# Low-rank projection of layers 1 and 3 with its weights stationary in two fp32r parts, in a four-layer convolution and feed-forward kernel

## The reference, cut to what matters

```python
x = x + _L0_ffn_ref(_L0_cond_ref(x, cond, ...), A, B, Wr, br)
x = x + _L1_ffn_ref(_L1_cond_ref(x, cond, ...), gate, kernel, bias, lora_A, lora_B, lora_A_shared, lora_B_shared)
x = x + _L2_ffn_ref(_L2_cond_ref(x, cond, ...), base_W, gate_W, lora_A, lora_B)
x = x + _L3_ffn_ref(_L3_cond_ref(x, cond, ...), W, b, A, Bmat, LiMEs)

def _L1_ffn_ref(x, gate, kernel, bias, lora_A, lora_B, lora_A_shared, lora_B_shared):
    base_out = jnp.matmul(x, kernel) + bias
    A_eff = jnp.einsum('bn,nri->bri', gate, lora_A)        # 32 columns, chosen by group of 4 samples
    B_eff = jnp.einsum('bn,nor->bor', gate, lora_B)
    Ax = jnp.einsum('bri,bti->btr', A_eff, x_flat)
    delta_flat = jnp.einsum('bor,btr->bto', B_eff, Ax)
    Ax_s = jnp.einsum('ri,bti->btr', lora_A_shared, x_flat)  # 32 columns, shared
    delta_flat = delta_flat + jnp.einsum('or,btr->bto', lora_B_shared, Ax_s)
    return base_out + delta_flat

def _L3_ffn_ref(x, W, b, A, Bmat, LiMEs):
    H = jnp.einsum('btd,od->bto', x, W) + b
    z = jnp.einsum('btd,dr->btr', x, A)                    # 32 columns
    ...                                                    # routing weights p_mix from H, z and LiMEs
    return H + jnp.einsum('btr,ro->bto', z * p_mix, Bmat) * scaling
```

## Time and profile before

| | |
|---|---|
| median of 3 executions | 1951.31 us (1949.11 to 1953.24) |
| span of the profiled execution, first to last instruction | 1944.8 us |
| TensorE busy in it | 1829.3 us (94%) |
| VectorE, ScalarE busy | 874.8 us (45%), 667.7 us (34%) |
| mean granted TensorE clock | 0.966 |

### The profile page before, as it was taken

The page is one execution under the profiler, slowest core; times in us unless marked ns, Lnnn a source line. Parts: engine busy times, 40 slices in busy tenths (PEclk is TensorE's granted clock), DMA queues, the critical chain, the costliest instruction groups (busy, mean ns, idle before and its releaser), DMA issues.

```text
span 1944.8 us, 28665 instructions
## 1 busy us (share of the span) xinstructions
PE 1829.3 (94%) x9728; PEld 1520.9 (78%) x9728; DVE 874.8 (45%) x2573; ACT 667.7 (34%) x1237; POOL 96.2 (5%) x173
## 2 busy tenths in 40 slices
PE   5889998979999999999899999999989999999995
PEld 4777787767888888887788888888767888888873
DVE  5155555644333333455543444444563333333327
ACT  2355555433333323325333222332253323332310
POOL 2000000010000000010000000000100000010000
PEclk9889999969999999999999999999999999999996
DMA  6565666436323322325322222221242222222218
GB/s 121 126 147 143 149 151 162 108 93 95 81 70 86 79 67 74 78 67 129 88 70 73 59 67 62 74 73 42 68 114 54 73 62 74 80 77 62 63 43 324
DMA packets 229831, 181.27 MB, mean 93 GB/s; under 512 B 178648, under 2 KB 189944, under 8 KB 229534
## 3 DMA queue, kind: packets, MB, share of 16 engines
q1 hardware_dynamic: 222142, 173.35, 34.7%
q10 hardware_dynamic: 2640, 5.26, 0.9%
q0 software_dynamic: 5008, 2.14, 0.9%
HBM read 108.34 MB, written 42.99 MB: 78 GB/s over the span
## 4 chain that ended last, share of the span: by engine, by line
PE 78%; issue 9%; DVE 4%; SPq 3%; DMA 3%; ACT 2%; POOL 0%; POOLq 0%; DVEq 0%; ACTq 0%
PE ps L970 64%; PE ps L1784 4%; PE ps L1055 3%; SPq L1321 3%; PE ps L1103 2%; DMA filt<-filt 2%; PE ps L1046 1%; ACT w_hi L1448 1%; PE ps L1804 1%; DVE x_last L1939 0%; POOL limes_rep L1864 0%; DVE filt L745 0%; DMA raw<-in_x 0%; PE ps L1996 0%; DMA raw<-in_L_ffn_base_W 0%
## 5 line engine op out<-in xcount | busy, mean ns | idle before, releaser
L970 PE MATMUL ps<-xp_hi,filt 128*128 128x512 f32 x1024 | 332.3, 406 | 13.5 <-DMA filt<-filt 12.0
L970 PE MATMUL ps<-w_hi,y_hi 128*128 128x512 f32 x768 | 314.1, 409 | 0.0
L970 PE MATMUL ps<-w_hi,y_lo 128*128 128x512 f32 x768 | 306.7, 399 | 0.0
L970 PE MATMUL ps<-w_lo,y_hi 128*128 128x512 f32 x768 | 305.8, 398 | 0.0
L970 PEld LDWEIGHTS ps<-xp_hi,filt 128*128 128x128 f32 x1024 | 187.2, 190 | 54.4 <-DMA filt<-filt 13.7
L734 DVE SCALAR_TENSOR_TENSOR xp_lo<-ps,mods_pair,xp_hi 128x512 fp32r<-128x512 f32 x128 | 96.2, 752 | 289.2 <-ACT xp_hi L403 289.1
L403 ACT ACTIVATE xp_hi<-ps,mods_pair 128x512 fp32r<-128x512 f32 x128 | 88.3, 690 | 379.9 <-PE ps L970 379.9
L970 PE MATMUL ps<-xp_lo,filt 128*128 128x512 f32 x512 | 202.5, 396 | 0.0
L970 PEld LDWEIGHTS ps<-w_lo,y_hi 128*128 128x128 f32 x768 | 146.2, 190 | 35.7
L419 ACT ACTIVATE y_nat<-ps,mods_pair 128x512 f32<-128x512 f32 x128 | 99.6, 778 | 215.3 <-PE ps L970 215.3
L970 PEld LDWEIGHTS ps<-w_hi,y_hi 128*128 128x128 f32 x768 | 147.3, 192 | 31.7
(11 more groups left out here) (313 smaller groups left out, 3096.9 us busy)
## 6 DMA issues: line engine op xcount, KB each, us to landing
x_in<-x_state SPq DMA_DIRECT2D x96, 256.0 KB, 3.8
x_res<-x_state SPq DMA_DIRECT2D x48, 512.0 KB, 4.0
x_state<-x_res SPq DMA_DIRECT2D x46, 512.0 KB, 2.9
filt<-filt SPq DMA_DIRECT2D x128, 128.0 KB, 2.7
filt<-filt SPq DMA_DIRECT2D x128, 96.0 KB, 2.4
raw<-in_x SPq DMA_DIRECT2D x16, 512.0 KB, 4.9
x_res<-in_x SPq DMA_DIRECT2D x16, 512.0 KB, 4.0
x_state<-raw SPq DMA_DIRECT2D x16, 512.0 KB, 3.5
```

The costliest lines, as they stand in the source:

```text
L970: ins = nc.tensor.matmul(out, st[x0], mv[x1], start=first and t == 0, stop=last and t == 2, **kw)
```

## The change

In layers 1 and 3 the projection's weights become stationary and the two parts of y move, so the result is z transposed, 64 partitions by 128 columns, and needs no transpose. The weights are held split in `proj_hi`. In layer 1, 64 high and 64 low columns are used in an `mm3` (24 fp32r matmuls for 8 blocks, 64-column stationary, 128 columns moving); in layer 3, 32 high and 32 low columns lie side by side as one stationary operand and each part of y moves once (16 matmuls), and the two halves of the result are added on ScalarE and VectorE. `y_f`, its wait, the copy to `z_sb` and the transpose fall away there; `y_lo` is made from PSUM. The mixed columns are loaded a pair earlier, ahead of the filter shifts of j = 0, and are split once for each iteration at the end of step j = 1; the fills of layers 1 and 3 split the first ones. Layers 0 and 2 compute as before.

```diff
-Z_OPS = (5, 1, 16, 1)
+Z_OPS = (5, 0, 16, 0)
@@ sp_step
+            if l == 1 and j == 0 and more:
+                load_mixed_a(sp, i + 1)
             if more:
                 sp_shift_filter(sp, l, n + 2)
             if l == 1 and j == 1 and more:
-                load_mixed(sp, i + 1)
+                load_mixed_b(sp, i + 1)
@@ act_split_y
-                if l != 2:
+                if l == 0:
                     nc.scalar.activation(y_f[:, :, C * q:C * q + C], src, ACT.Copy).then_inc(s["act_f"], 1)
@@ act_step
-            if l in (1, 2):
+            if l > 0:
                 act_tail_in(act, l, n)
+            if l == 1 and j == 1:
+                split_adapter_act(act, i + 1)
@@ dve_y_lo
-                if l == 2:
-                    src = ps[:, 3 + 2 * q, :].rearrange("p (b c) -> p b c", c=C)
-                else:
-                    dve.wait_ge(s["act_f"], whole_y(l, n, q))
-                    src = y_f[:, :, c]
+                src = ps[:, 3 + 2 * q, :].rearrange("p (b c) -> p b c", c=C)
@@ dve_step
                 dve_tail_in(dve, l, n)
+            if l == 1 and j == 1:
+                split_adapter_dve(dve, i + 1)
@@ pe_step (and pe_drain)
-            if l in (1, 3):
-                pe.wait_ge(s["act_f"], whole_y(l, n, 1))
@@ act_narrow, dve_narrow (fill of layer 3)
+                nc.scalar.activation(proj_hi[:, :, 0:32], proj_raw[:, :, 0:32], ACT.Copy).then_inc(s["adapt_act"], 1)
...
+                dve.wait_ge(s["adapt_act"], GROUPS + 1)
+                nc.vector.tensor_tensor(proj_hi[:, :, 32:C], proj_raw[:, :, 0:32], f(proj_hi[:, :, 0:32]),
+                                        ALU.subtract).then_inc(s["adapt_dve"], 1)
@@ dve_shared, act_shared (fill of layer 1)
             last.then_inc(s["shared_ready"], 1)
+            dve.wait_ge(s["adapt_act"], 1)
+            v.tensor_tensor(proj_hi[:, :, C:2 * C], proj_raw[:], f(proj_hi[:, :, 0:C]), ALU.subtract).then_inc(s["adapt_dve"], 1)
             dve.wait_ge(s["base_act"], 1)
...
             act.wait_ge(s["shared_ready"], 1)
+            act.wait_ge(s["adapt_loaded"], 16)
+            nc.scalar.activation(proj_hi[:, :, 0:C], proj_raw[:], ACT.Copy).then_inc(s["adapt_act"], 1)
@@ new
+        def split_adapter_act(act, g):
+            act.wait_ge(s["adapt_loaded"], 16 * g + 16)
+            act.wait_ge(s["pe_zt"], pid(1, 2 * g))
+            nc.scalar.activation(proj_hi[:, :, 0:32], proj_raw[:, :, 0:32], ACT.Copy).then_inc(s["adapt_act"], 1)
+
+        def split_adapter_dve(dve, g):
+            dve.wait_ge(s["adapt_act"], g + 1)
+            nc.vector.tensor_tensor(proj_hi[:, :, C:C + 32], proj_raw[:, :, 0:32], f(proj_hi[:, :, 0:32]),
+                                    ALU.subtract).then_inc(s["adapt_dve"], 1)
@@ act_tail_in, dve_tail_in
+            if l == 3:
+                act.wait_ge(s["dve_zt"], pid(l, n))
+                nc.scalar.activation(z_sb[0:32, 0:P], ps[32:C, 6, 0:P], ACT.Copy).then_inc(s["act_zt"], 1)
+                return
...
             if l == 3:
-                dve.wait_ge(s["pe_zt"], pid(l, n) + 1)
-                v.tensor_copy(zt_nat[:, ds(P * n, P)], ps[0:96, 6, 0:P]).then_inc(s["dve_zt"], 1)
+                for c in range(3):
+                    last = v.tensor_tensor(zt_nat[32 * c:32 * c + 32, ds(P * n, P)], ps[0:32, 6, 0:P], z_sb[0:32, 0:P], ALU.add)
+                last.then_inc(s["dve_zt"], 1)
@@ dve_route
-            if l == 1:
-                done(v.tensor_copy(z_sb[:, 0:PROJ_W[l]], ps[:, 6, 0:PROJ_W[l]]), 1)
-            if l == 3:
-                done(v.tensor_copy(z_sb[:, 0:96]...), 1)
@@ pe_project
+            if l == 1:
+                if j == 0:
+                    pe.wait_ge(s["adapt_dve"], i + 1)
+                for kb in range(KB):
+                    last = mm3(ps[0:C, 6, 0:P], [proj_hi[:, kb, 0:C], proj_hi[:, kb, C:2 * C]],
+                               [t[:, kb] for t in (y_hi, y_lo)], kb == 0, kb == KB - 1)
+                last.then_inc(s["pe_zt"], 1)
...
+            if l == 3:
+                for kb in range(KB):
+                    for r, t in enumerate((y_hi, y_lo)):
+                        last = mm(ps[0:C, 6, 0:P], proj_hi[:, kb, 0:C], t[:, kb], start=kb == 0 and r == 0, stop=kb == KB - 1 and r == 1)
+                last.then_inc(s["pe_zt"], 1)
@@ pe_project_T
+            if l in (1, 3):
+                return
```

More of the change, by code:

```diff
@@ L219, in build @@
             dve_mp dve_g dve_t dve_y dve_x dve_b dve_l dve_p dve_end dve_k dve_z dve_zt dve_o dve_e
-            x_loaded e_loaded chain""".split()
+            x_loaded e_loaded chain adapt_loaded adapt_act adapt_dve""".split()
         s = {n: sem(n) for n in names}
@@ L1550, in pe_wide @@
                 pe.wait_ge(s["raw_dve"], part_count(l, NARROW_PARTS[l] + 15))
+            if l == 3:
+                pe.wait_ge(s["adapt_dve"], GROUPS + 1)
         def act_wide(act, l):
@@ L1653, in mix_store, with load_mixed_a, load_mixed_b @@
                     .then_inc(s["mix_stored"], 16)
-        def load_mixed(sp, g):
+        def load_mixed_a(sp, g):
             if is_zero(g):
                 sp.wait_ge(s["mix_stored"], 5 * 16)
+            else:
+                sp.wait_ge(s["adapt_dve"], g)
+            sp.dma_start(proj_raw[:, :, 0:32], mixed_a_dram[g].rearrange("p (k r) -> p k r", r=32)).then_inc(s["adapt_loaded"], 16)
+        def load_mixed_b(sp, g):
+            if is_zero(g):
                 sp.wait_ge(s["narrow_pe"], 1)
@@ L1727, in dve_route @@
                                             z_small[:, 16:24].unsqueeze(2).to_broadcast([P, 8, 16]), ALU.mult, ALU.mult), 5)
-            if l == 1:
-                done(v.tensor_copy(z_sb[:, 0:PROJ_W[l]], ps[:, 6, 0:PROJ_W[l]]), 1)
-            if l == 3:
-                done(v.tensor_copy(z_sb[:, 0:96].rearrange("p (c r) -> p c r", c=3),
-                                   ps[:, 6, 0:32].unsqueeze(1).to_broadcast([P, 3, 32])), 1)
             if l == 2:
@@ L1776, in pe_project @@
         def pe_project(pe, l, i, j):
-            n = 2 * i + j
-            if l == 1 and j == 0:
-                pe.wait_ge(s["mixed_loaded"], 32 * i + 32)
-            if l != 2:
-                proj = proj_0 if l == 0 else proj_raw
+            mm = nc.tensor.matmul
+            if l == 0:
                 for kb in range(KB):
-                    last = nc.tensor.matmul(ps[:, 0 if l == 0 else 6, 0:PROJ_W[l]], y_f[:, kb], proj[:, kb, 0:PROJ_W[l]],
-                                            start=kb == 0, stop=kb == KB - 1)
+                    last = mm(ps[:, 0, 0:PROJ_W[l]], y_f[:, kb], proj_0[:, kb], start=kb == 0, stop=kb == KB - 1)
                 last.then_inc(s["pe_z"], 1)
-                return
-            for kb in range(KB):
-                last = mm3(ps[:, 6, 0:PROJ_W[l]], [t[:, kb] for t in (y_hi, y_lo)],
-                           [t[:, kb, 0:PROJ_W[l]] for t in (proj_hi, proj_lo)], kb == 0, kb == KB - 1)
-            last.then_inc(s["pe_z"], 1)
+            if l == 1:
[5 more added lines that the diff above has]
+                last.then_inc(s["pe_zt"], 1)
+            if l == 2:
+                for kb in range(KB):
+                    last = mm3(ps[:, 6, 0:PROJ_W[l]], [t[:, kb] for t in (y_hi, y_lo)],
+                               [t[:, kb, 0:PROJ_W[l]] for t in (proj_hi, proj_lo)], kb == 0, kb == KB - 1)
+                last.then_inc(s["pe_z"], 1)
+            if l == 3:
+                for kb in range(KB):
+                    for r, t in enumerate((y_hi, y_lo)):
+                        last = mm(ps[0:C, 6, 0:P], proj_hi[:, kb, 0:C], t[:, kb], start=kb == 0 and r == 0, stop=kb == KB - 1 and r == 1)
+                last.then_inc(s["pe_zt"], 1)
         def pe_ffn(pe, l, n, h):
@@ L2023, in _ @@
                 if l == 0:
-                    load_mixed(sp, 0)
+                    load_mixed_a(sp, 0)
+                    load_mixed_b(sp, 0)
                     load_kernel(sp, 1)
```

21 lines of the change are left out of this document (8 added, 13 removed).

## The result

The changed kernel takes 1921.13 us (median of 4, 1916.96 to 1923.92) and the kernel before beside it 1952.28 (4 runs, 1949.11 to 1955.01): a ratio of 0.9833, 95% interval 0.9813 to 0.9854, 31.2 us faster by the medians and 32.6 by the ratio. The prediction was 1922.4. The nearness is in part luck: two errors of opposite sign stand behind it, and both can be read in the traces.

What follows compares the result with a forecast made beforehand. TensorE, busy throughout steady layers 1 and 3, was taken as the bound. Projection and transpose 25.6, clock 3.1 and ends 0.2 make 28.9 us off 1951.3: 1922.4, range 1917 to 1938.

Steps and rivals of the forecast that it cites:

- term 1: Projection in layers 1 and 3: new instructions at 0.060 us each, gaining 0.44 and 0.92 us a pair.
- Rival A: New projection instructions: load and stream hide each other only in part, 0.085 us each, time 1938.4; chance 0.14.
- rival B: New projection instructions cost what full ones cost, 0.111 to 0.118 us; 1955.1 to 1962.6; chances 0.05 and 0.08.
- 0.05 of the exit: End of the new projection: 0.05 us added because the next w_hi's full load hides only behind one 0.060 instruction.
- term 2: Transpose of z between the last fb matmul and second w_hi, layers 1 and 3: removal gains 0.12 us a pair.
- term 3: Clock drops to 0.50 after the projection at two pairs of steady layer 3: both gone, 3.1 us gained.
- term 4: Ends of layers: last pairs of layers 3 and 1 gain 0.9 us, layer 1's fill loses 0.7; net 0.2.
- Edits at nothing: Side work on ScalarE, VectorE and SyncE, such as y_f, splits, z's chain and the moved load: hidden behind waits, costing nothing.
- The base: Whole kernel: the median stands 6.5 us above the profiled span, and the gain is carried over unchanged to 1951.3.

Runs made afterwards that it cites:

- experiment 2: Kernel before, with layer 3's projection matmul streaming 64 columns instead of 32, the added ones unused: 1946.83 us against 1953.48, ratio 0.9976.
- p3_long: Changed kernel; layer 1 32 stationary by 64 moving columns, layer 3 64 by 32 with each matmul issued twice; layer 1 0.032 us per instruction, no run time given.
- p2_moving: Changed kernel, 64 stationary columns kept, moving columns cut from 128 to 64 in layer 1 and 32 in layer 3; 0.058 us per instruction, no run time given.

## Why the prediction was right, and where it wasn't

**Price of an instruction (term 1): right.** 0.059 to 0.060 was predicted as 0.060, for the reason given. Rival A (0.085) and rival B (0.105 and more) did not occur. The sentence of the Trainium skill, "TensorE: Matmul & The Clock Gate", "Back-to-back issue gap", on 81 ns for a pair of load and matmul at 128 columns, does not agree with this case's traces: 0.060 with 64 or 32 stationary columns and 0.111 with 128. The group of transposes at 0.111 was no guide either, though its shape was the same; it moves unsplit fp32. That the load did not set its price could be read before: the transposes of y, unsplit too and with 128 stationary columns, are no further apart, (1.04 - 0.28) / 7 = 0.109 in this row of the kernel before:

```profile
557.22 1.04 PE L1103 MATMUL ps<-ident,y_nat 128*128 128x128 f32 x8
```

It also has the shape of which the prediction said that no row has it; for fp32r that was so.

**The block's gain (term 1): mis-sized by 0.08 to 0.09 a pair.** The prediction set the start of the first w_hi matmul at 596.86 - 0.233 = 596.63. The trace of before has a row for it that I had not used:

```profile
596.55 0.48 PE L970 MATMUL ps<-w_hi,y_hi 128*128 128x512 f32 x1
596.86 0.39 PE L970 MATMUL ps<-w_hi,y_lo 128*128 128x512 f32 x1
```

The distance behind it is 0.315, not 0.233. The old block from gu_lo to w_hi was 2.025, in both layers, and is now 1.703 in layer 1 and 1.221 in layer 3: gains of 0.32 and 0.80. The distance behind w_hi is now 0.29 and 0.28 and not 0.315 and 0.320, 0.03 more: 0.35 and 0.84 where 0.44 and 0.92 were predicted. The 0.05 of the exit was booked as new though the old exit had cost more.

**The transpose (term 2): right for half of the steps.** 0.12 in the steps without edges: 0.35 + 0.12 makes the 0.46 by which the step of 26.71 falls to 26.25. In the steps with edges the matmul behind the transpose was 0.318 away and is now 0.340, and 0.06 is left: 29.97 to 29.57. With layer 3's 0.97 and 0.88 the 32 pairs give 8 x (0.46 + 0.40 + 0.97 + 0.88) = 21.7 us, not 25.6.

**The clock (term 3): 3.1 right, its place too narrow, its cause half right.** The two drops in steady layer 3 are gone in all seven traces of kernels with the change there. At the old length they come with 32 columns and not with 64 (experiment 2), but with 32 columns they came behind 1.9 us of them and not behind 1.0 (`p3_long`, `p2_moving`), so in the steady part the new projection would have kept the clock with 32 as well. Why the clock falls behind the one and not the other no run here shows. What failed is that I looked for the lower clock in the steady part alone. The rows of the last pair showed a projection of 3.62 us where 1.97 is the rule, which is the lower clock, and I read only its wait. That drop, 6.8 us at 0.50, is worth up to 3.4; two more at the end of layer 1, 3.4 us and 6.8 us, up to 5.1. So the clock gave up to 11.6 us and not 3.1; the table, less the steps and the ends below and without layer 2, leaves 32.8 - 21.7 - 0.4 = 10.7 for it. This covers the 3.9 us that the steps gave too little. It is a net sum: the fill of layer 2 has stretches at 0.50 too, 3.4, 3.4 and 10.2 us in the three traces with the old layer 1 and 6.8 or 10.2 in the five with the new, at a place where TensorE waits much of the time.

**The ends (term 4): right.** Last pair of layer 3: from its first transposes to the projection 3.61 before, 2.76 now, 0.85 against 0.6; TensorE's wait fell from 2.52 to 1.67. Last pair of layer 1: the same distance fell from 3.55 to 3.34, 0.2 against 0.3. Fill of layer 1: 0.63 lost against 0.7, shown by undoing it; the wait there is 5.34 in the first trace, where the matmuls ahead of it met a later drop of the clock and ended sooner, and 4.5, as predicted, in both repeats. VectorE's subtraction cost nothing there, as its idle time fell from 4.18 to 3.40. Layer 3's fill shows no cost that stands out of 62.1 to 64.4.

**Edits at nothing: right.** In steady layers 1 and 3 TensorE shows no wait for the split weights, for z or for the tail. ScalarE still waits 7.23 us for the transposes in a step of layer 1, where it was 7.16, and VectorE 5.46 us for the tail, where it was 5.53:

```profile
591.93 1.22 DVE L829 TENSOR_TENSOR x_res<-ps,x_res 128x1024 f32<-128x1024 f32 x1 [5.46 <-PE ps L971]
592.27 1.09 ACT L430 ACTIVATE y_hi<-ps 128x512 fp32r<-128x512 f32 x2 [7.23 <-PE ps L1104]
```

SyncE's waits for the filter are 539.8 us in 63 times, 562.4 before, so the moved load hides in them. ScalarE's busy time fell by 24.3 us, not 35: the group of `y_f` by 38.6, while `z_sb` (16 copies, 4.3 us) and the splits (3.9) came in; the other 6 I did not attribute.

**The base.** The prediction took the 6.5 us between the median and the span of before as fixed. With the profiled execution's own time known, it is 1.7 us in each of the kernels after (1921.90 and 1920.2 for the first). The profiled execution of before was therefore some 4.8 us quicker than its median. Carrying the difference over was the right choice; taking the span as the kernel's time would not have been.

**The range.** It was said to take in rival A's price, but A's sum gives 1938.4 and the range ends at 1938. Nothing hung on it.

## What to carry to other kernels

Where TensorE is the bound and a matmul is small, count both sides: for fp32r here an instruction cost the longer of its load and its stream, 0.058 us for 64 stationary columns and 0.060 for 128 moving, so turning a thin product round to 64 by 128 halves what each costs. Take the distances at both ends of a block from the rows, not from the rule of the middle. And price the granted clock over the whole span, its ends among it: here 16 records of 32 columns, 1.9 us long, were followed at two of the steady pairs of layer 3 by 3.4 us at half the clock, and removing them won that back too.

## What was not expected of the hardware

- Streaming 64 columns instead of 32 in the 16 records of each projection of layer 3, for nothing, made the kernel before faster (0.9976, 0.9960 to 0.9991); in its trace the granted clock in the steady steps behind them no longer fell to 0.50.
- The same 32 moving columns left the clock at 1.00 in steady layer 3 when the projection took 1.0 us and not when it took 1.9. In the last pair, where TensorE waits as well, it fell in both.
- Nearly all of the scatter between the profiled executions lies ahead of layer 1 and in the fills: layer 1's first transposes start anywhere from 440.6 to 451.1 us in 13 traces (441.9 to 451.1 without the two that have the shorter fill), while a steady step of layers 1 to 3 repeats to 0.03 us across kernels that share its code. A step read from one trace settled 0.05 us, where 5 to 12 timed runs left intervals of 6 to 11 us.
- A gain can come with a drop of the clock somewhere else: with 4.4 us taken out of layer 1's fill, a drop of 3.4 us stood behind layer 1's last pair, twice of twice, and in none of the five traces with the new layer 1 and the longer fill.
